# The condition term copied into the gates' bank by ScalarE, products on constants in rounds 0 to 2, and layer norm's mean product ahead of its variance product

## The reference

```python
x = x + L0_attn(LSTM(x, h0=cond))           # linear attention over the 8 sequences, 16 heads
x = x + L0_ffn(tanh_RNN(x, h0=cond))        # 16 experts of width 128, top 2 of each 32-wide head
x = x + L1_attn(LSTM(x, h0=cond))           # layer norm, softmax attention, 8 heads
x = x + L1_ffn(GRU(video=cond, seq=x))      # 8 experts and a shared one, top 4
```

```python
a = x_t @ Wx + b + h @ Wh;  i, f, o = sigmoid(a[0:3]);  g = tanh(a[3])
c = f * c + i * g;  h = o * tanh(c)
```

```python
vz, vr, vh = cond @ C_z + b_z, cond @ C_r + b_r, cond @ C + b      # the condition term: one value per gate row and sequence
z = sigmoid(x_t @ W_z + h @ U_z + vz);  r = sigmoid(x_t @ W_r + h @ U_r + vr)
hh = tanh(x_t @ W + (r * h) @ U + vh);  h = (1 - z) * h + z * hh
```

## Time and profile before

| | |
|---|---|
| median of 3 runs | 2633.78 us (2632.69 to 2638.45) |
| profiled execution | 2631.72 us |
| its span in the profile | 2629.9 us |
| TensorE busy | 2355.9 us, 90% of the span |
| VectorE busy | 1897.1 us, 72% |
| ScalarE busy | 1206.2 us, 46% |
| GpSimd busy | 163.9 us, 6% |
| HBM traffic over the span | 18 GB/s |

### The profile page before, as it was taken

One profiled execution on the slowest core, in us unless ns is written; L12 is line 12 of the kernel. 1 busy time (PEld: TensorE's weight loads), 2 busy tenths in 40 slices (PEclk: granted clock), 3 DMA queues, 4 the chain that ended last, 5 costly groups with the idle time before them and its releaser, 6 DMA issues. The chain is left out here.

```text
span 2629.9 us, 114287 instructions
## 1 busy us (share of the span) xinstructions
PE 2355.9 (90%) x47776; PEld 1959.4 (75%) x47776; DVE 1897.1 (72%) x7976; ACT 1206.2 (46%) x3950; POOL 163.9 (6%) x157
## 2 busy tenths in 40 slices
PE   3778899999999999998776875999999999999999
PEld 2556677777777777764444664999999999999998
DVE  5757777777777777788856666777777777777775
ACT  3225555555555555556635663333333333333333
POOL 0000000000000000000004940000000000000000
PEclk8668999999999999999967885999999999999999
DMA  6000000000000000011002332000000000000000
GB/s 190 2 2 2 5 5 5 5 5 5 5 3 5 5 5 5 5 45 28 4 4 69 109 79 81 7 9 11 9 9 9 10 11 9 9 9 9 5 5 6
DMA packets 53179, 53.37 MB, mean 20 GB/s; under 512 B 25126, under 2 KB 47288, under 8 KB 50746
## 3 DMA queue, kind: packets, MB, share of 16 engines
q1 hardware_dynamic: 47878, 30.57, 4.3%
q0 software_dynamic: 1728, 12.58, 1.4%
q10 hardware_dynamic: 3060, 2.90, 0.4%
HBM read 39.46 MB, written 6.57 MB: 18 GB/s over the span
## 5 line engine op out<-in xcount | busy, mean ns | idle before, releaser
L2026 PE MATMUL p<-xn,m_h 128*128 128x128 f16 x6144 | 619.0, 219 | 0.0
L2026 PE MATMUL p<-xn,m_l 128*128 128x128 f16 x3072 | 551.5, 219 | 0.0
L2026 PEld LDWEIGHTS p<-xn,m_h 128*128 128x128 f16 x6144 | 483.4, 97 | 0.8
L867 ACT ACTIVATE gl<-gt 128x128 f32<-128x128 f32 x324 | 100.2, 309 | 598.0 <-DVE gt L1065 597.2
L607 PE MATMUL lg_b<-xn,lh 128*32 128x256 f16 x6144 | 300.1, 291 | 77.2 <-DVE lh L1089 69.1
L1065 DVE STREAM_TRANSPOSE gt<-lg_b 128x512 f32<-128x512 f32 x324 | 230.1, 710 | 181.0 <-PE lg_b L607 180.3
L882 ACT ACTIVATE hm<-xy,b 128x512 f32<-128x512 f32 x512 | 347.9, 680 | 0.0
L2026 PEld LDWEIGHTS p<-xn,m_l 128*128 128x128 f16 x3072 | 299.2, 97 | 1.7
L2046 PE MATMUL po<-m_h,xn 128*128 128x256 f16 x1536 | 293.1, 273 | 1.8 <-DVE xn L2197 1.4
L607 PEld LDWEIGHTS lg_b<-xn,lh 128*32 128x32 f16 x6144 | 159.9, 101 | 161.1 <-DVE lh L1089 117.5
L607 PE MATMUL lg_b<-e_wh_hi,lh 128*32 128x256 f16 x4096 | 210.1, 283 | 30.6 <-DVE lh L1089 30.0
(11 more groups left out here) (400 smaller groups left out, 5931.7 us busy)
## 6 DMA issues: line engine op xcount, KB each, us to landing
m_stage<-in_m_w POOLq DMA_DIRECT2D x12, 1024.0 KB, 5.4
hs<-in_m_w SPq DMA_DIRECT2D x16, 384.0 KB, 3.3
x_dram<-x SPq DMA_DIRECT2D x16, 128.0 KB, 2.1
xs<-in_l_wv SPq DMA_DIRECT2D x1, 2048.0 KB
attention_dram<-att SPq DMA_DIRECT2D x16, 128.0 KB, 2.8
xn<-x_dram SPq DMA_DIRECT2D x16, 128.0 KB, 2.5
xn<-attention_dram SPq DMA_DIRECT2D x128, 16.0 KB, 1.8
out_dram<-xn SPq DMA_DIRECT2D x16, 128.0 KB, 2.2
```

Source lines behind the costliest of these rows:

```text
L867: act.activation(gl[:, :].rearrange("p (m b) -> p m b", b=B), gt[:, :].rearrange("p (m n) -> p m n", n=32)[:, :, slot % QS * B:(slot % QS ...
L2026: last = pe.matmul(banks[mat][:, j * CW:(j + 1) * CW], w[:, mat, k, GM * slot + j, :], g[:, par, k, :], start=(q % 18 == 0), stop=(q % 6 = ...
```

## The change

1. `keep_busy`: at the end of each slot of steps 0 to 45 TensorE makes products of 512 columns of a vector of ones with a part of a weight matrix, into a bank that nobody reads and that `w1` overwrites from step 46 on: 6 in a slot of round 0, 2 in slots 0 to 10 of rounds 1 and 2, 5 in slots 11 and later, 180 in all.
2. Layer norm in part one: TensorE makes the mean of unit u before the variance of unit u-1; VectorE subtracts the mean (`norm_center`) and makes `norm_low` after the LSTM's state instead of before it.
3. Part three: VectorE adds `vt_h` and `vt_l` once into `vt32` in float32; ScalarE copies `vt32`, repeated over 8 steps (128x384), into the bank of the gates, in slot 0 for the second half and in slot 10 for the first half of the next chunk, and `project_half` leaves out the 12 products of L1884 (in 31 of its 32 calls; the very first keeps them) and waits for this copy.

```diff
+            def keep_busy(i, slot):
+                if i * C + slot >= FIRST_STEP["w1"]:
+                    return
+                for _ in range(6 if i == 0 else 5 if slot > 10 else 2):
+                    pe.matmul(xy[0][:, :], ones2[:, :], w_hi["a_wh"][:, 0, 0:512], start=True, stop=True)
...
+                if unit_at(i, slot, 0) is not None:
+                    norm_mean(unit_at(i, slot, 0))
                 if unit_at(i, slot, 1) is not None:
                     norm_var(unit_at(i, slot, 1))
-                if unit_at(i, slot, 0) is not None:
-                    norm_mean(unit_at(i, slot, 0))
                 if pair_at(i, slot, 0) is not None:
                     norm_spread(pair_at(i, slot, 0))
+                keep_busy(i, slot)
...
+                if slot == E0 and i > LAG:
+                    dve.wait_ge(e_kept, 2 * (i - LAG))
+                state(i, slot)
                 if unit_at(i, slot, 0) is not None:
                     norm_center(unit_at(i, slot, 0))
                 if pair_at(i, slot, 1) is not None:
                     norm_low(pair_at(i, slot, 1))
-                if slot == E0 and i > LAG:
-                    dve.wait_ge(e_kept, 2 * (i - LAG))
-                state(i, slot)
...
-        def project_half(pe, half):
+        def project_half(pe, half, preset):
...
-                for v in (vt_h, vt_l):
+                for v in () if preset else (vt_h, vt_l):
                     pe.matmul(o, ident_h[:, :], v[:, m, :].unsqueeze(1).to_broadcast([P, 8, B]), start=first,
                               stop=False, skip_group_check=True)
...
                     if slot == 2:
-                        if i > 0:
-                            pe.wait_ge(low_clear, i * C)
-                        project_half(pe, 1)
+                        pe.wait_ge(preset, 2 * i + 1)
+                        project_half(pe, 1, True)
                     if slot == 12 and scans(i + 1):
                         pe.wait_ge(x3_split, 2 * (i + 1))
-                        pe.wait_ge(low_clear, i * C + 8)
-                        project_half(pe, 0)
+                        pe.wait_ge(preset, 2 * i + 2)
+                        project_half(pe, 0, True)
...
+            def preset_gates(i, half):
+                if half == 0:
+                    act.wait_ge(u_added, i * C + 8)
+                elif i > 0:
+                    act.wait_ge(u_added, i * C)
+                else:
+                    act.activation(g_b[1][:, GATES:GATES + 6 * B], zeros[:, :], ACT.Copy)
+                act.activation(g_b[half][:, 0:GATES].rearrange("p (s n) -> p s n", s=8),
+                               vt32[:, :].unsqueeze(1).to_broadcast([P, 8, 6 * B]), ACT.Copy).then_inc(preset, 1)
...
                 silu(i, slot)
+                if slot == 0 and scans(i):
+                    preset_gates(i, 1)
+                if slot == 10 and scans(i + 1):
+                    preset_gates(i, 0)
```

More of the change, by code:

```diff
@@ L1813, in pipeline_two @@
         zeros = sb("zeros", [P, 6 * B])
+        vt32 = sb("vt32", [P, 6 * B])
         h32 = sb("h32", [P, 16])
@@ L1839, in pipeline_two @@
             sem(n) for n in ("hid_pe", "th_act", "uw_done", "a_done", "a_hi3", "a_lo3", "w3_pe", "po_free"))
+        preset = sem("preset")
         z_full, z_free = sem("z_full3"), sem("z_free3")
@@ L1943, in _ @@
             def _(pe):
-                project_half(pe, 0)
+                project_half(pe, 0, False)
+            @block.vector
+            def _(dve):
+                flat = "p m b -> p (m b)"
+                dve.tensor_tensor(vt32[:, :], vt_h[:, :, :].rearrange(flat), vt_l[:, :, :].rearrange(flat),
+                                  ALU.add).then_inc(cleared, 1)
         block = ctx.enter_context(nc.Block())
```

## The result

The changed kernel takes 2598.0 us (median of 4 runs, 2594.3 to 2603.3) where the kernel before took 2634.1 us in the same comparison: a ratio of 0.9866, with a 95% interval of 0.9842 to 0.9890. The direction is the forecast's; the gain is 36 us where I had summed up 25 us. The profiled execution has a span of 2592.5 us, against 2629.9 us.

A forecast was written before the change was run, and what follows sets the result against it. Part one was taken as a chain through all engines with TensorE often idle, part three as TensorE-bound. -9.5 - 4.5 - 11.2 = -25.2 us took 2631.72 to 2606.5 us, so 2608.6 us for the median, range 2598 to 2623.

The forecast's parts named there:

- more than forecast: Rival: the clock is held throughout rounds 0 to 2 and A reaches its far bound; 2601 us, chance 0.10.
- A: Products on constants in rounds 0 to 2 of part one raise TensorE's clock: -9.5 us, bounds -3 and -16.
- B: Layer norm's new order in part one, so the state needs no mean: -4.5 us, bounds 0 and -7.
- The clock is not held: Rival: two constants per slot are too few in rounds 1 and 2; A about -3 us, 2615 us, chance 0.20.
- the 20%: Slot 4, full of float32 scores, went from 6.49 us in round 1 to 5.18 us in round 3 despite more work.
- What is late next is TensorE itself, about 5.1 us at this clock: Layer norm step of part one: with the subtraction behind the state, TensorE's work sets the length, about 5.1 us.
- C: Condition term of part three, 12 products fewer per call of `project_half`: -11.2 us, bounds -9 and -12.
- so all of it shows: Part three: TensorE bounds the slot with the call, so the full 0.35 us saved per call shortens it.
- issue-bound rival: Rival: issue bounds small products on TensorE; A gives 0, B 4.5 us, C's calls 23 us; 2606 us, chance 0.02.
- Attention: Layer 1's attention, between B and C: a shift in time may change the clock there, 1 to 2 us either sign.

The follow-up runs named there:

- the second comparison: The changed kernel run again beside more runs of the kernel before: 2597.1 us (5 runs) against 2633.7 us (11 runs), ratio 0.9866.
- `b_clock`: Kernel before, old orders, plus three constant products of 512 columns in each of steps 303 to 311; round 19 took 63.3 us, against 69.9.
- the comparison of the single parts: Kernel before with only A, B or C added: 2622.9, 2617.5 and 2621.5 us, against a median of 2627.0 us for the kernel before.
- `hold_more`: Changed kernel plus three constant products per step from 303 on and four per slot in round 0 of part three; 2605.6 us, against 2597.1.

## Why the prediction was right, and where it was not

The forecast was 2608.6 us in a range of 2598 to 2623, and the median of 2598.0 us lies at the very edge of that range; 2597.1 us, the median of the second comparison, lies outside it. It is closer to the rival "more than forecast" (2601 us; its bound of -16 gives 2602) than to the forecast, but not for that rival's reason, a clock held throughout in A. Two of the three terms were about right; the extra came from B's clock and, in the first pair, from luck.

**A, forecast -9.5 us.** The first profile showed -12.4. Over all profiles, rounds 0 to 2 take 187.3 to 190.8 us in the six without constants, mean 188.8, and 176.7 to 181.2 in the six with A as written, mean 179.8: -9.0 us. The term holds, and the first profile was a good draw. Its inner split was off: round 0 gave 3.8 us on the mean where I had 1.5, since its slots 3, 4, 7, 8 and 9 gained 0.4 to 0.7 us each, not 0.3; rounds 1 and 2 gave 5.3 us and not 8, because the level still falls in single slots. "The clock is not held" was the right thing to fear: slot 4 of round 1, from which I had read the 20%, took 6.42 to 6.50 us in five of the six profiles with A, as before, and 4.95 us only in the first. One reading was wrong and changes nothing in the sum: the LSTM's 24 products have 256 columns each (128x256), not 64. In the timeline of the kernel before they start four at a time (each of the four has a `tile_position` of its own), and the fours follow each other after 0.11 us at 2.4 GHz and 0.21 us at 1.2 GHz. So the 35 and 61 ns are averages over four that run side by side, and no price of one product; that all 24 take 0.84 us still excludes 62 ns for each.

**B, forecast -4.5 us.** Measured -9.5, outside my bounds of 0 and -7: 86.5 us without B (mean of four profiles that keep all of B's old order and add nothing there), 77.0 with it (six). The step that failed is the sentence "What is late next is TensorE itself, about 5.1 us at this clock". The clock was held fixed in my sum while I removed TensorE's idle time, and it did not stay: steps 304 to 310 have a granted clock of 0.73 in the kernel before and 0.93 to 1.00 in the six profiles with B, where steps 308 and 309 take 3.1 us. That holding the clock up is enough to shorten them is what `b_clock` shows; whether they would take 5.1 us in the new order at 1.2 GHz, no run shows. The order itself measures 2.5 to 4.0 us in steps 304 to 310, a little below my 4.5. I had weighed the clock for A, where the change speaks of it, and not for B, where it came as a consequence.

**C, forecast -11.2 us.** Measured -9.5 us in part three in the first pair, -9.3 us in the means of the four profiles with C as it is and the seven without it. The price of a call (1.05 us), of slot 12 (4.64) and of the copy (0.48) came out within 0.01 us, and round 0's two calls gave 1.25 us for 1.1. The failed step is "so all of it shows". I had read it from slot 12 and applied it to slot 2, where nine routing operations on VectorE were the next thing late, and 0.24 us of 0.35 was lost in each clean round, about 3.4 us in all; some rounds gave 0.2 to 0.4 us back where single slots (2, 6, 14 and others) had been longer before. The issue-bound rival is out: 36 products of a call take 1.05 us, 29 ns each. The 62 ns that the Trainium skill gives for a matmul with decoding in hardware off (page "TensorE: Matmul & The Clock Gate", section "Wait — 56ns, not 53.3ns?") do not show in this trace.

**Attention, forecast 1 to 2 us of either sign.** It gave 5.8 us in the pair of profiles, and it is chance: 173.3 to 179.8 us over fourteen profiles with the same instructions in that stage, with no order by what was changed (mean 175.4 us in the six with all three parts, 175.9 in the eight others). The mechanism was named and its size was three times too small. Rounds 16 to 18 have another such step of 1.2 to 1.5 us.

**The sum.** The three measured parts make -28 us, close to my -25; the 36 us of the two comparisons need some 8 us more. The stretches of the first pair of profiles account for it (A's good draw 3.4, attention 5.8, rounds 16 to 18 1.2, less B's 0.7). In the two comparisons themselves it is not settled: by means the whole is at -36.5 and -34.4 us there, and at about -31 us if it is held against the 2628.7 us of the kernel before in the comparison of the single parts, so 3 to 6 us of what the stretches leave open lie in the base and not in the changed kernel.

## What to carry to other kernels

Where a profile shows the lower clock level, ask of every edit that removes or adds TensorE idle time whether it moves the level, and cost the stretch at both: here a reordering worth 2.5 to 4 us at equal level brought 9.5. Constant products pay where they fill idle time that really is idle; behind a waiting product, or where TensorE's list is full, they cost their full length. And a saving read off one slot holds for another only if the same engine ends last in both.

## What the runs showed of the hardware

- The same program, with the same instructions, has a stretch that lasts between 173 and 180 us as TensorE's level falls at one place or another (granted clock 0.89 and 0.85). The kernel before ranged from 2620.9 to 2638.2 us with a clock of 0.947 down to 0.936, and its median moved by 7 us between comparisons. A difference below some 7 us is better read from stretches of the trace than from medians here.
- Two products of 512 columns in a slot of 3 us (five from slot 11 on) brought the clock of rounds 1 and 2 from 0.67 and 0.69 to 0.83 to 0.96 in six profiles; the same count with 64 columns left it at 0.69 and 0.75.
- In round 0 of part three TensorE was busy 80% of the time in `hold_more` (46.9 of 58.4 us) and still had a clock of 0.61, where round 1 of the changed kernel has 76% (43.4 of 57.3 us) and 0.96: busy share alone does not tell the level.
- The same order of layer norm's steps 304 to 310 took 33.5 us at a granted clock of 0.73 and 26.8 us at 1.00, with three products on constants added to each step.
